# Moving the second unit's queries and the folded biases ahead of the first scores' read-out

## The reference, cut to what matters

```python
xn = _layernorm(x)
s = _L0_attn_ref(xn, ...)              # windows of 64 tokens, 16 heads, relative bias, softmax
g = _silu(_L0_ffn_ref(xn, ...))        # top-1 of 32 experts, at most 160 tokens each
x = x + s * g
xn = _layernorm(x)
s = _L1_attn_ref(xn, ...)              # fft based; its weights are folded with a DFT beforehand
g = _silu(_L1_ffn_ref(xn, ...))        # top-2 of 8 experts
x = x + s * g
```

## Time and profile before

| | us |
|---|---|
| median of 3 runs | 1129.23 (1128.43 to 1129.9) |
| the profiled execution, its own time | 1124.32 |
| its span | 1122.5 |
| PE busy | 1027.6 (92%) |
| DVE busy | 692.4 (62%) |
| ACT busy | 531.8 (47%) |
| POOL busy | 404.1 (36%) |

### The profile page before, as it was taken

The page is one execution under the profiler, slowest core; times in us unless marked ns, Lnnn a source line. Parts: engine busy times, 40 slices in busy tenths (PEclk is TensorE's granted clock), DMA queues, the critical chain, the costliest instruction groups (busy, mean ns, idle before and its releaser), DMA issues.

```text
span 1122.5 us, 16791 instructions
## 1 busy us (share of the span) xinstructions
PE 1027.6 (92%) x6152; PEld 883.9 (79%) x6152; DVE 692.4 (62%) x1488; ACT 531.8 (47%) x1101; POOL 404.1 (36%) x385
## 2 busy tenths in 40 slices
PE   3876999999999984789999999999999999999995
PEld 2665788888888863578888898988888888888884
DVE  7777876777777759588845644474765200058853
ACT  4624655555555536743444545455453223356531
POOL 1056545454555440000243322332231245522364
PEclk9969999999999996987999999999999999999998
DMA  9932345546565338426496855544234579989971
GB/s 307 287 136 81 94 134 164 171 133 190 179 210 174 103 109 264 157 93 254 98 350 241 290 188 187 185 171 188 108 130 191 213 269 340 338 294 389 390 285 63
DMA packets 120401, 228.65 MB, mean 204 GB/s; under 512 B 14938, under 2 KB 103914, under 8 KB 115328
## 3 DMA queue, kind: packets, MB, share of 16 engines
q1 hardware_dynamic: 106448, 189.31, 48.7%
q0 software_dynamic: 13872, 38.27, 10.3%
HBM read 166.98 MB, written 62.79 MB: 205 GB/s over the span
## 4 chain that ended last, share of the span: by engine, by line
PE 72%; DVE 14%; ACT 5%; issue 3%; POOL 2%; DMA 2%; SPq 0%; POOLq 0%; DVEq 0%; ACTq 0%
PE PS L1318 20%; PE PS L1308 20%; PE PS L1207 6%; PE PS L1092 4%; PE PS L1042 4%; PE PS L1146 3%; PE PS L1217 2%; PE PS L1173 2%; PE PS L1101 2%; PE PS L1159 2%; PE PS L1184 2%; POOL table L2327 2%; DVE stats L1349 2%; PE PS L1294 1%; DVE hot_tile L1831 1%
## 5 line engine op out<-in xcount | busy, mean ns | idle before, releaser
L1308 PE MATMUL PS<-xgT,WE 128*128 128x256 f32 (+1 forms) x1248 | 254.7, 361 | 5.0 <-ACT hT L2284 4.3
L2284 ACT ACTIVATE hT<-PS,WE 128x256 f32<-128x256 f32 (+1 forms) x312 | 140.2, 455 | 227.0 <-PE PS L1308 224.1
L1308 PEld LDWEIGHTS PS<-xgT,WE 128*128 128x128 f32 x1248 | 219.3, 190 | 33.3 <-ACT hT L2284 6.6
L1318 PE MATMUL PS<-WE,hT 128*128 128x256 f32 x1104 | 244.6, 379 | 0.0
L1318 PEld LDWEIGHTS PS<-WE,hT 128*128 128x128 f32 x1104 | 207.4, 190 | 27.0
L1943 DVE TENSOR_TENSOR y<-PS,WE 128x512 f32<-128x512 f32 (+1 forms) x38 | 24.3, 640 | 211.1 <-PE PS L1318 211.1
L2384 POOL DMA_INDIRECT xg<-xn_dram,token_of x71 | 74.2, 1045 | 136.9 <-DVE result_of L1859 115.1
L2396 POOL DMA_INDIRECT result<-y,result_of x53 | 53.7, 1013 | 175.7 <-DVE y L1943 168.5
L1042 PE MATMUL PS<-XT,Wf 128*128 128x256 f32 x384 | 91.6, 393 | 3.3 <-ACT Z L2061 3.3
L1042 PEld LDWEIGHTS PS<-XT,Wf 128*128 128x128 f32 x384 | 73.7, 197 | 14.6 <-ACT Z L2061 4.9
L2343 POOL TENSOR_TENSOR prob<-prob,row_sum 128x512 f32<-128x512 f32 x56 | 58.6, 1046 | 59.5 <-DVE row_sum L1525 59.2
(11 more groups left out here) (280 smaller groups left out, 1714.4 us busy)
## 6 DMA issues: line engine op xcount, KB each, us to landing
WE<-in_experts SPq DMA_DIRECT2D x39, 2180.0 KB, 9.7
wgu<-in_w_gate SPq DMA_DIRECT2D x32, 256.0 KB, 2.9
wgu<-in_w_up SPq DMA_DIRECT2D x32, 256.0 KB, 3.2
wdn<-in_w_down SPq DMA_DIRECT2D x32, 256.0 KB, 3.9
result<-zeros SPq DMA_DIRECT2D x16, 512.0 KB, 5.0
xs<-late_dram SPq DMA_DIRECT2D x16, 512.0 KB, 13.5
both<-result SPq DMA_DIRECT2D x16, 512.0 KB, 8.3
table<-zeros POOLq DMA_DIRECT2D x1, 5160.0 KB, 31.1
```

Of the source, the lines that this page charges most:

```text
L1308: m = e.matmul(PS[:, FIRST_H_BANK + nth % HR, 0:rows], W1[n % WR][:, k, c * P:(c + 1) * P], xgT[:, n % 2, k, 0:rows], start=k == 0, stop=k ...
L1318: m = e.matmul(PS[:, u.bank, j * D:(j + 1) * D], hT[:, n % 2, c, j * P:(j + 1) * P], W2[n % WR][:, c, :], start=c == 0, stop=c == KF - 1)
L2284: e.activation(hT[:, n % 2, c, 0:rows], PS[:, FIRST_H_BANK + (KF * n + c) % HR, 0:rows], ACT.Gelu_apprx_tanh, bias=b1[n % WR][:, c:c + 1], ...
```

## The change

After the counts' products, and before the first step's scores are read out, PE's list now has the queries of unit 1 (tiles 2 and 3), the value bias product and the folded biases. The small product `fold_bias_terms` on DVE is put ahead of `route0_center`. The generator `routing` is gone. In unit 0 the keys of unit 1 are made in step 0 and its values in step 1; in the other units nothing is moved.

```diff
         add("route0_best")
         add("route0_hot")
+        add("fold_bias_terms")
         for n in range(3):
             for c in range(KD):
                 fold(n, c)
...
         add("route0_center")
         route0_count()
+        q(1)
+        fold_v_bias()
+        fold_biases()
         scored(0)
         need(("score_out", 0))
         add("route0_gate")
         need(("exp", 0))
         add("route0_put")
+        need(("q_out", 1))
+        need(("fold_biases_out",))
         scored(1)
         need(("score_out", 1))
+        need(("fold_v_bias_out",))
         need(("exp", 1))
-
-    def routing():
-        add("fold_bias_terms")
-        fold_v_bias()
-        yield
-        fold_biases()
-        yield
...
     def side(half):
-        if advance(route):
-            wanted = (half - 2 * FIRST_EXPERT_STEP + 1) * EXPERT_PIECES // (2 * (LAST_EXPERT_STEP - FIRST_EXPERT_STEP))
-            while pieces[0] < min(wanted, EXPERT_PIECES + 1):
-                advance(ffn)
-                pieces[0] += 1
+        wanted = (half - 2 * FIRST_EXPERT_STEP + 1) * EXPERT_PIECES // (2 * (LAST_EXPERT_STEP - FIRST_EXPERT_STEP))
+        while pieces[0] < min(wanted, EXPERT_PIECES + 1):
+            next(ffn, None)
+            pieces[0] += 1
...
-        if u + 1 < UNITS and g < 3:
+        if u == 0 and g < 2:
+            (k, v)[g](1)
+        elif 0 < u < UNITS - 1 and g < 3:
             (q, k, v)[g](u + 1)
```

More of the change, by code:

```diff
@@ L418, in combination @@
         need(("route1_turn_out", 4 * QUARTERS - 8))
-    def advance(generator):
-        return next(generator, generator) is generator
-    route, ffn, pieces = routing(), experts(), [0]
+    ffn, pieces = experts(), [0]
     def side(half):
-        if advance(route):
-            wanted = (half - 2 * FIRST_EXPERT_STEP + 1) * EXPERT_PIECES // (2 * (LAST_EXPERT_STEP - FIRST_EXPERT_STEP))
-            while pieces[0] < min(wanted, EXPERT_PIECES + 1):
-                advance(ffn)
-                pieces[0] += 1
+        wanted = (half - 2 * FIRST_EXPERT_STEP + 1) * EXPERT_PIECES // (2 * (LAST_EXPERT_STEP - FIRST_EXPERT_STEP))
+        while pieces[0] < min(wanted, EXPERT_PIECES + 1):
+            next(ffn, None)
+            pieces[0] += 1
     start()
@@ L448, in schedule0 @@
             pturn(s)
-    assert next(ffn, None) is None and next(route, None) is None
+    assert next(ffn, None) is None
     order.settle(order.clock + STEPS * UT)
```

## The result

| | before | changed |
|---|---|---|
| median of 9 runs each, us | 1129.23 | 1133.62 |
| fastest and slowest | 1123.94, 1130.84 | 1131.85, 1139.3 |
| span of the profiled execution | 1122.5 | 1130.8 |

Ratio of the changed kernel to the kernel before: 1.0059, 95% interval 1.0044 to 1.0075, so 6.7 us slower (5.0 to 8.5). Measured once more beside later experiments it was 1.0061 (1.0038 to 1.0084). The ratio compares runs of the same chips; the medians alone, 4.4 us apart, mix them.

The account below looks back on a forecast made before the run. Up to 109.5 us a chain bounds the kernel: DVE's routing, indices, 32 POOL writes, step 8's subtraction. Indices +5.8 us, all else 0, on 1129.23 gives 1135.0 us; own range 1133.5 to 1138, widened to 1132 to 1138.5.

Parts of the forecast that it names:

- The forecast case: Indices, and so step 8's subtraction, come 5.8 us late and the whole kernel with them: 1135.0 us; chance 68%.
- Order on PE: Moved queries (1.73 us) and v-bias product (1.03 us) run at full clock behind the counts' products, ending at 58.33.
- Order on DVE, the deciding step: DVE stands at the v-bias read-out until 58.4, so the gate sum begins at 60.9, not 55.12: indices +5.8 us.
- POOL's writes: The same 32 indirect writes begin 5.8 us later; change in their waits for landing taken as 0, 0.5 us either side.
- Attention covered: Attention up to 5.9 us late at the scatter's end, within 12.4 us of room, so it costs nothing.
- The clock: PE may stand idle longer before the scatter's end and return at a lower clock: 0 to 1.9 us, taken as 0.
- The gap is filled: Rival: 8.0 us of PE work fills the idle gap, everything behind comes up to 8 us earlier, 1121 us; chance 5%.
- The read-out stands elsewhere: Rival: v-bias read-out behind route0_put on DVE, or its product early enough; gate sum stays at 55.1, 1129.2 us; chance 9%.
- Partly given back: Rival: PE's 29 us idle between 400 and 500 us return half of the delay, 1132 us; chance 8%.

Follow-up runs that it names:

- experiment 1: Changed kernel with the v-bias read-out on DVE put behind the indices and the first read-out of step 1; 1131.91 us, ratio 0.9981 to the kernel before.
- experiment 3: Kernel before with only the v-bias product moved, directly behind the counts' products, its read-out again first on DVE; 1138.49 us, ratio 1.0037.
- experiment 4: Kernel before with nothing moved, but six extra fills of a free buffer on DVE ahead of the gate sum; 1139.55 us, ratio 1.0047.
- experiment 2: Kernel before with only the queries of unit 1 moved (keys and values one step up), both bias products left in place; 1132.01 us, ratio 0.9979.
- experiments 5 to 8: Kernel before again, 1.0007; with POOL and experts first needed at step 12: order of experiment 1 1.0047, changed kernel 1.0106, kernel before 1.0060.
- the three with later use: Experiment 1's order, changed kernel and kernel before, POOL first needed at attention step 12 instead of 8, experts at 12 instead of 9; 1133.46, 1140.53, 1134.56 us.

## Why the prediction was right

It said 1135.0 us, 5.8 us slower; measured were 1133.62, and by the ratio 6.7 us (5.0 to 8.5) slower. The forecast case held. That the sum came so near is in part luck: the profiles show its one large term as forecast (5.62) and a second one of 1.9 us that it had put at 0, outside the 0.5 us it allowed.

- *Order on PE.* Queries 1.89 us, v-bias product 1.03 us and over at 58.71 (57.68 + 1.03); predicted were 58.33, and the opening of this profile was 0.39 later. The full clock in the stretch held, granted 0.98 from 56 to 62 us.
- *Order on DVE, the deciding step.* Read-out at 58.75 directly behind the product, 6.40 us of standing, gate sum at 61.13 (60.9 predicted, to which the 0.39 come again). The delay is 61.13 - 55.12 - 0.39 = 5.62 us against 5.8. Experiments 1, 3 and 4 show it as the cause: without the read-out in that place no loss, with it alone a loss of 4.2 us, and a loss of 5.3 us from a plain delay of DVE.
- *POOL's writes.* The one term that was mis-sized. I took their change as 0 with 0.5 us to either side; from indices to step 8's subtraction it was 50.17 and 50.50 us in two profiles of the changed kernel, against 48.26 and 48.24 in two of the kernel before, 1.9 to 2.3 us more. The waits for landing were 8.2 us instead of 7.1, one of them 3.5, and single writes took up to 1466 ns instead of 1306 (on average 1015 ns instead of 988, 0.9 us in all). So the last write began at 116.3 and step 8's subtraction at 117.40, where 114.2 and 115.3 were predicted:

```profile
L2325 POOL DMA_INDIRECT table<-XN,slot_put x32: 971/976/1466, 68.1 to 116.3; - x32
...
  DMA table<-XN,slot_put: 8.2, 3
```

What lengthened them was not tried. The waits for landing were 8.2, 8.4 and 8.2 us in all three profiles of the changed order with its three pauses, the longest each time 3.5 to 3.8 us, and 6.9 to 7.2 us in all others with three pauses, experiments 1, 3 and 4 among them. So it is neither PE's list alone nor the late start alone.
- *Attention covered.* Step 8's maximum was ready at 108.30 instead of 102.84, 5.5 us late, within the 5.9 I allowed, and POOL began at 117.40: 9.1 us of room. The cover held. That products in the gap are not worth their time on PE is shown by experiments 1 (8 us moved) and 2 (4 us moved), which gained at most 0.36% and 0.37%.
- *The clock.* PE did stand longer and came back at the low level (granted 0.63 from 121 to 124 us, where the kernel before had 1.00); this cost nothing that shows, as the stretch from step 8's subtraction to the last tail product is 301.48 against 301.63 us. The value 0 was right; that DVE and POOL set the pace there is the reason given, and no run tests it by itself.
- *The rivals.* "The gap is filled" is refuted: it was right on the granted clock in the filled gap (0.98), wrong on the time, as the gap opened again behind it, at 0.50. The advice that the prediction took from the Trainium skill (TensorE: Matmul & The Clock Gate, section Why this matters for your kernels), to leave no idle gaps between bursts of matmuls because the clock falls, agrees with the trace on the clock and not on the time. "The read-out stands elsewhere" is not what happened, but experiment 1 is that rival as a kernel, and its time was as it said: not slower than the kernel before. "Partly given back" did not occur.

## What to carry to other kernels

Where all engines walk one plan, moving a product moves its read-out too, and on an in-order engine the read-out holds everything behind it: look up, on each engine, which item stands directly behind the moved one and who waits for that. Filling the busiest engine's gap is worth little (here at most 0.4%) while another chain, here indices, 32 writes and one subtraction, ends later. Before work is given from one engine to another to use a wait, see how full the other is: in experiments 5 to 8 DVE, with four more steps of POOL's work, was busy 13.47 of 14 us.

## What the runs showed of the hardware that was not expected

With fewer pauses between POOL's indirect writes the other engines stood longer. With three pauses of some 2.4 us among 32 writes ACT and DVE had waits on "remote" between 40 and 140 us of 0 us (kernel before twice, the changed kernel's first profile, experiment 1, the three with later use), 5.6 (experiment 2), 6.9 (the changed kernel again), 8.9 (experiment 3) and 13.9 us in all (experiment 4). With one pause they had 16.0 to 44.1 us in all (13.4 + 10.0 + 7.7 + 5.9 = 37.0 in the kernel before), and that kernel was 13 us slower (ratio 1.0118) though its writes were done sooner. All three with one pause ran on one chip, on which the changed kernel with three pauses had 6.9 us of them against 44.1 with one. The waits view of the kernel before with shorter writes:

```profile
ACT bf L2136 <- remote: 13.4, 1, 13.4
DVE KB L1485 <- remote: 10.0, 1, 10.0
...
ACT OT L2172 <- remote: 7.7, 1, 7.7
```

What "remote" is remains open. The page of every kernel lists DMA queues of kind "instruction", and a load of an engine's next instructions that cannot get through while POOL issues without a pause would fit; no run here shows it. The Trainium skill, Runtime: NRT & Kernel Launch, section Instruction fetch mechanics, says that each engine's sequencer fetches its next block of instructions by a DMA queue of its own and that this is mostly hidden. If these waits are that fetch, then it was not hidden here, by 13.4 us. Not every wait ended at a pause of POOL (the third above did not), so the pauses are not the whole of it.

A second point: the opening, the same work in all these kernels but for one DVE product of 0.14 us that some have in it, ended (router's exponentials over) at 55.1 to 61.2 us. Even two profiles of one kernel differ: 55.09 and 55.28 for the kernel before, 55.48 and 57.14 for the changed one. In the latest, experiment 2, the products of unit 0's values began 3.2 us later on PE than in the first profile of the kernel before (43.62 against 40.42), and the folding of the weights took 7.5 us instead of 5.48, with a granted clock of 0.50 from 50 to 54 us instead of 1.00. What makes an opening late was not tried. So profiles of two kernels are to be compared from a common event, not from zero.
